# A drain behind the products of TensorE's walk: who raises the counts

## The reference, cut to what matters

```python
xn = layernorm(x)
# 1. graph part: mean over the neighbours, one product, norm
nsum = segment_sum(xn[src], dst, 6250);  deg = segment_sum(1, dst, 6250)
g = relu(concat([xn, nsum / max(deg, 1)]) @ W + b);  g = g / max(|g|, eps)
# 2. mixing: linear attention over all nodes, 4 heads of 32
q, k, v = split(rmsnorm(xn, g_pre) @ w_qkv)          # + 4 memory keys and values
q = softmax(q, over a head's 32) * scale;  k = softmax(k, over the nodes)
context = k^T v  (32 x 32 per head);  mix = rmsnorm((q context) @ w_out + b_out, g_out) + xn
x = x + g + mix
# 3. eight experts, the top two per node: gelu(ln(x) @ W1 + b1) @ W2 + b2, weighed and added
out = x + experts(layernorm(x))
```

## Time and profile before

| what | number |
|---|---|
| timed, median of 3 runs | 1981.92 us (1981.72 to 1984.41) |
| the profiled execution: its span | 2187.4 us |
| busy, share of that span: TensorE | 1583.7 us, 72% |
| VectorE | 1101.1 us, 50% |
| GpSimd | 1140.4 us, 52% |
| ScalarE | 900.9 us, 41% |

### The profile page before, as it was taken

How to read it: one execution, slowest core, us unless ns; L and a number is a source line. 1 busy time by engine, 2 the same in 40 slices (tenths; PEclk the granted TensorE clock), 3 DMA queues, 4 the chain that set the end, 5 groups by cost and what they waited for, 6 DMA issues and landing times.

```text
span 2187.4 us, 33907 instructions
## 1 busy us (share of the span) xinstructions
PE 1583.7 (72%) x9422; PEld 1361.2 (62%) x9423; DVE 1101.1 (50%) x3043; ACT 900.9 (41%) x1840; POOL 1140.4 (52%) x1141
## 2 busy tenths in 40 slices
PE   6735536546566667867767763548999999999998
PEld 5524435435454544545545543447999999999997
DVE  6512212212234536655555457765666666666664
ACT  6501101101112323323334336554666666666664
POOL 3267666666656666666666612555333333333333
PEclk9868868767878979988888785558999999999999
DMA  7334333333324655566656526537878777877775
GB/s 210 119 100 114 104 101 107 101 97 103 106 81 154 224 165 182 182 180 184 198 182 189 181 76 197 188 135 248 228 215 220 213 221 208 226 214 221 213 221 137
DMA packets 188123, 368.85 MB, mean 169 GB/s; under 512 B 33324, under 2 KB 134172, under 8 KB 173656
## 3 DMA queue, kind: packets, MB, share of 16 engines
q0 software_dynamic: 77296, 252.50, 41.3%
q1 hardware_dynamic: 102992, 113.64, 16.3%
q10 hardware_dynamic: 7736, 1.52, 0.4%
HBM read 287.94 MB, written 80.39 MB: 168 GB/s over the span
## 4 chain that ended last, share of the span: by engine, by line
PE 50%; another core or an unknown queue 17%; DVE 12%; issue 11%; DMA 5%; ACT 3%; SPq 2%; POOL 0%; DVEq 0%; ACTq 0%; POOLq 0%
PE bank L1813 11%; PE bank L2002 5%; PE bank L2003 5%; PE bank L2004 5%; PE bank L2025 5%; PE bank L2024 5%; PE bank L2026 5%; PE bank L1879 3%; DMA xTs<-xnT_d 3%; PE bank L1830 2%; PE bank L1973 1%; DVE acc_lent L1478 1%; DMA z_d<-w2s_lent 1%; DVE acc_lent L1307 1%
## 5 line engine op out<-in xcount | busy, mean ns | idle before, releaser
L695 POOL DMA_INDIRECT w2s_lent<-z_d,edge_tabs_lent x784 | 777.5, 992 | 438.7 <-issue 256.7
L1307 DVE TENSOR_TENSOR acc_lent<-acc_lent,bank 128x258 f32 x244 | 102.7, 421 | 600.6 <-remote 348.8
L1813 PE MATMUL bank<-w2s_lent,S_lent 128*128 x976 | 261.0, 416 | 19.0 <-issue 9.5
L1031 ACT ACTIVATE G<-bank,acc_lent 128x256 f32<-128x256 f32 x448 | 188.3, 472 | 205.9 <-DVE w2s L1670 124.5
L1813 PE MATMUL bank<-w2s_lent,G 128*128 x976 | 265.9, 422 | 3.4 <-issue 3.4
L2024 PE MATMUL bank<-w2s 128*128 128x256 f32 x896 | 264.4, 295 | 0.0
L2002 PE MATMUL bank<-w2s,acc 128*128 128x256 f32 x896 | 260.4, 291 | 2.8 <-issue 2.8
L739 POOL DMA_INDIRECT out_dram<-G,acc_lent x112 | 179.6, 1604 | 158.3 <-DVE G L1650 117.3
L1629 DVE TENSOR_TENSOR acc<-w1s,acc 128x512 fp32r<-128x512 f32 x224 | 155.1, 693 | 200.7 <-ACT acc L1000 174.1
L2004 PE MATMUL bank<-w2s,acc 128*128 128x256 f32 x896 | 254.0, 284 | 0.0
L2025 PE MATMUL bank<-w2s 128*128 128x256 f32 x896 | 253.7, 283 | 0.4 <-issue 0.4
(11 more groups left out here) (322 smaller groups left out, 2993.3 us busy)
## 6 DMA issues: line engine op xcount, KB each, us to landing
w2s<-w_d POOLq DMA_DIRECT2D x112, 1024.0 KB
w_d<-w2s_lent SPq DMA_DIRECT2D x64, 256.0 KB
acc_lent<-bucket_d SPq DMA_DIRECT2D x56, 266.0 KB
w2s_lent<-z_d,edge_tabs_lent POOLq DMA_INDIRECT x784
bu_d<-w2s_lent SPq DMA_DIRECT2D x98, 128.0 KB
w2s_lent<-bu_d SPq DMA_DIRECT2D x14, 768.0 KB
w1s<-in_L_ffn_W_dram SPq DMA_DIRECT2D x8, 1024.0 KB
w2s_lent<-in_L_ffn_W_dram SPq DMA_DIRECT2D x32, 256.0 KB
```

What stands on the lines that cost most here:

```text
L695: pool.indirect_dma_start(out=ring_rows[:, row % (RING * QUAD), 0:D], out_offset=None, in_=z_d[:, :], in_offset=bass.IndirectOffsetOnAxis( ...
L1031: g = act.activation(raw[q % 2][:, k * MT:(k + 1) * MT], bank[q][:, k * MT:(k + 1) * MT], ACT.Gelu, bias=b1c[1 - par][:, 2 * q + k:2 * q + ...
L1307: dve.tensor_tensor(to, to, bank[j % DEPTH][:, 0:ACCW], ALU.add).then_inc(s["acc_done"], 1)
L1813: m = pe.matmul(bank[j % DEPTH][:, 0:ACCW], S_of[j % DEPTH][:, k, :], rows[:, ds(bases[j], ACCW)], start=(k == 0), stop=(k == QUAD - 1))
```

## The change

A drain is an instruction in TensorE's stream that is done when all before it on that engine is done. At each of the places of the walk and the mixing where the last product of a group raised a semaphore, that product no longer does; a drain behind it does. All calls of `follow()` are left out (its function remains, without a caller). Nothing else changes: the same products in the same order, the same counts and waits. In the core of the diff (`turn_a`, `kv`, `ctx_mm`, `qu`, `bfold` and the turned biases are changed in the same way as `turn`; `kmaxrowT`, `ctxT` and `M2` as `kmaxT`):

```diff
@@ turn @@
                 for k in range(QUAD):
                     rows = ring[:, k * ACCW:(RING - 1) * QW_RING + (k + 1) * ACCW]
-                    m = pe.matmul(bank[j % DEPTH][:, 0:ACCW], S_of[j % DEPTH][:, k, :], rows[:, ds(bases[j], ACCW)],
+                    pe.matmul(bank[j % DEPTH][:, 0:ACCW], S_of[j % DEPTH][:, k, :], rows[:, ds(bases[j], ACCW)],
                                   start=(k == 0), stop=(k == QUAD - 1))
-                m.then_inc(s["p_ready"], 1)
-                if j < B_FIRST:
-                    follow()
+                pe.drain().then_inc(s["p_ready"], 1)
...
             def kv(t):
...
                 for c in range(DC):
-                    m = pe.matmul(bank[4][:, 0:2 * HID], xTs[:, c * P:(c + 1) * P], w_kv[:, c, :], start=(c == 0), stop=(c == DC - 1))
-                m.then_inc(s["kv_mm"], 1)
+                    pe.matmul(bank[4][:, 0:2 * HID], xTs[:, c * P:(c + 1) * P], w_kv[:, c, :], start=(c == 0), stop=(c == DC - 1))
+                pe.drain().then_inc(s["kv_mm"], 1)
...
-            pe.transpose(bank[6][:, 0:P], kmax, ident[:, :]).then_inc(s["kmaxT"], 1)
-            follow()
+            pe.transpose(bank[6][:, 0:P], kmax, ident[:, :])
+            pe.drain().then_inc(s["kmaxT"], 1)
...
             pe.matmul(bank[7][:, 0:D], ctxT, w_outs, start=True, stop=True)
-            follow(4)
+            pe.drain().then_inc(s["M2_mm"], 1)
...
             def turn_q(t):
                 pe.wait_ge(s["q_ready"], t + 1)
-                pe.transpose(bank[6][:, 0:P], q_s, ident[:, :]).then_inc(s["qT_mm"], 1)
+                pe.transpose(bank[6][:, 0:P], q_s, ident[:, :])
+                pe.drain().then_inc(s["qT_mm"], 1)
 
             def mix_out(t):
                 pe.wait_ge(s["qT_sb"], t + 1)
                 until(pe, s["o_evac"], t)
-                pe.matmul(bank[7][:, 0:D], qT_s, M2[:, :], start=True, stop=True).then_inc(s["o_mm"], 1)
+                pe.matmul(bank[7][:, 0:D], qT_s, M2[:, :], start=True, stop=True)
+                pe.drain().then_inc(s["o_mm"], 1)
```

More of the change, by code:

```diff
@@ L1822, in turn_a @@
                 for c in range(DC):
-                    m = pe.transpose(bank[5][:, c * P:(c + 1) * P], xr[:, c * P:(c + 1) * P], ident[:, :])
-                m.then_inc(s["xaT_mm"], 1)
+                    pe.transpose(bank[5][:, c * P:(c + 1) * P], xr[:, c * P:(c + 1) * P], ident[:, :])
+                pe.drain().then_inc(s["xaT_mm"], 1)
             def kv(t):
@@ L1843, in _ @@
             pe.wait_ge(s["kv_dve"], NT)
-            pe.transpose(bank[6][:, 0:P], kmax, ident[:, :]).then_inc(s["kmaxT"], 1)
-            follow()
+            pe.transpose(bank[6][:, 0:P], kmax, ident[:, :])
+            pe.drain().then_inc(s["kmaxT"], 1)
             pe.wait_ge(s["km_ready"], 1)
-            pe.transpose(bank[6][:, 0:P], kmaxb, ident[:, :]).then_inc(s["kmaxrowT"], 1)
-            follow()
+            pe.transpose(bank[6][:, 0:P], kmaxb, ident[:, :])
+            pe.drain().then_inc(s["kmaxrowT"], 1)
             pe.wait_ge(s["mk_exp"], 1)
@@ L1856, in ctx_mm @@
                 for j in range(nt):
-                    m = pe.matmul(bank[5][:, 0:HID + 2], ek[0:rows, j, :],
+                    pe.matmul(bank[5][:, 0:HID + 2], ek[0:rows, j, :],
                                   kv_all[0:rows, ds(8 * g + j, 1), HID:KVW].rearrange("p o w -> p (o w)"),
                                   start=False, stop=last, skip_group_check=True)
-                m.then_inc(s["ctx_mm"], 1)
+                pe.drain().then_inc(s["ctx_mm"], 1)
             for g in range(6):
@@ L1864, in _ @@
             ctx_mm(6, 1, TAIL, True)
-            follow()
             pe.wait_ge(s["ctx_ready"], 1)
-            pe.transpose(bank[6][:, 0:P], ctxs, ident[:, :]).then_inc(s["ctxT_mm"], 1)
-            follow()
+            pe.transpose(bank[6][:, 0:P], ctxs, ident[:, :])
+            pe.drain().then_inc(s["ctxT_mm"], 1)
             pe.wait_ge(s["ctxT_ready"], 1)
-            pe.matmul(bank[7][:, 0:D], ctxT, w_outs, start=True, stop=True).then_inc(s["M2_mm"], 1)
-            follow(4)
+            pe.matmul(bank[7][:, 0:D], ctxT, w_outs, start=True, stop=True)
+            pe.drain().then_inc(s["M2_mm"], 1)
             pe.wait_ge(s["M2_ready"], 1)
@@ L1878, in qu @@
                 for c in range(DC):
-                    m = pe.matmul(bank[4][:, 0:HID + D], xTs[:, c * P:(c + 1) * P], w_qu[:, c, :], start=(c == 0), stop=(c == DC - 1))
-                m.then_inc(s["qu_mm"], 1)
+                    pe.matmul(bank[4][:, 0:HID + D], xTs[:, c * P:(c + 1) * P], w_qu[:, c, :], start=(c == 0), stop=(c == DC - 1))
+                pe.drain().then_inc(s["qu_mm"], 1)
             def turn_q(t):
                 pe.wait_ge(s["q_ready"], t + 1)
-                pe.transpose(bank[6][:, 0:P], q_s, ident[:, :]).then_inc(s["qT_mm"], 1)
+                pe.transpose(bank[6][:, 0:P], q_s, ident[:, :])
+                pe.drain().then_inc(s["qT_mm"], 1)
             def mix_out(t):
@@ L1893, in bfold @@
                 for c in range(DC):
-                    m = pe.matmul(bank[5][0:EXPERTS, :], lnb[:, c, :], w1s[:, ds((e * DC + c) * HIDDEN + n * 512, 512)],
+                    pe.matmul(bank[5][0:EXPERTS, :], lnb[:, c, :], w1s[:, ds((e * DC + c) * HIDDEN + n * 512, 512)],
                                   start=(c == 0), stop=(c == DC - 1))
-                m.then_inc(s["bf_mm"], 1)
+                pe.drain().then_inc(s["bf_mm"], 1)
             for t in range(NT):
@@ L1913, in _ @@
                     for c in range(HC):
-                        m = pe.matmul(bank[5][:, c * EXPERTS:(c + 1) * EXPERTS], bacc[0:EXPERTS, c * P:(c + 1) * P], ident[0:EXPERTS, 0:EXPERTS],
+                        pe.matmul(bank[5][:, c * EXPERTS:(c + 1) * EXPERTS], bacc[0:EXPERTS, c * P:(c + 1) * P], ident[0:EXPERTS, 0:EXPERTS],
                                       start=True, stop=True)
-                    m.then_inc(s["b1_mm"], 1)
+                    pe.drain().then_inc(s["b1_mm"], 1)
             mix_out(NT - 1)
```

## The result

The changed kernel takes 2023.14 us (median of 4 runs, 2020.55 to 2029.48) against 1981.82 us before (4 runs, 1980.19 to 1984.41): 1.0216 times the time, 95% interval 1.0191 to 1.0240, or 41.3 us more. The forecast was 1992 us, 10 us more: the sign is right, and the loss is four times the forecast.

A forecast was written before the change was run, and what follows sets the result against it. The prediction took GpSimd's gathers to pace the walk; 4 us of lag left after mixing, 2 for the last chain and 4 of allowance made 10, on 1981.9: 1992 us. Its own range was 1986 to 2007, 8 in 10 1968 to 2035.

The forecast's parts named there:

- late counts: In the profiled walk before, TensorE's counts reached waiting engines late, once 39 us; the timed runs were taken to have few.
- The price of a drain: TensorE's cost per drain in walk and mixing: 0.44 us behind a turn, 0.36 behind another product.
- third cost: Sequencer work ahead of the next product now stands behind the drain: 0.13 us for a turn, 0.05 us elsewhere.
- fall by 23 x 0.9 to 4 at the end: Mixing's last 23 steps: TensorE's lag behind GpSimd falls 0.9 us a step, from 25 to 4 us.
- 16 x 1.3: Mixing's sixteen steps with a bfold: each takes TensorE 1.3 us more than the gathers, raising its lag from 4 to 25.
- C: Rival, chance 0.17: a drain is dearer, 0.6 us; mixing steps of 11.3 and 13.7 us add 63 us, 2045 us.
- A: Rival, chance 0.27: the gathers hide all of it at 0.31 us a drain; 1 to 2 us are left, 1983 us.
- B: Rival, chance 0.20: late counts cost something in the timed runs too, and drains' counts come in time: 1969 us.
- The tell-tale of C: Sign in the profile after that would show the dearer drain: GpSimd waits for L1813 through the mixing.
- where no gather runs: Stretch between the halves: counts come at once there, TensorE and the engines it waits for going round in 4.46 us.

The follow-up runs named there:

- e11: Kernel before with only two of a quad's four gathers from the ninth quad on: 1744.55 us, 0.8801 of the kernel before.
- e3: Kernel before without its 101 constant products and without any drain: 1979.92 us, 0.9991 of the kernel before.
- e1: Changed kernel with drains only up to the end of the stretch between the halves, no constant products: 1979.57 us, 0.9992 of the kernel before.
- e2: Kernel before, constant products kept, with drains raising the counts in the mixing only: 2022.64 us, 1.0223 of the kernel before.
- e7: Changed kernel with the register loads for the next eight turns issued ahead of the eighth turn's drain: 1992.55 us, 1.0072 of the kernel before.
- e9: Kernel before with drains only behind the mixing's products other than turns, register loads right behind every eighth turn's products: 1990.34 us, 1.0041 of the kernel before.
- e8: Changed kernel with two drains at each of the 517 places, the second raising the count: 2046.09 us, 1.0339 of the kernel before.
- e10: Kernel before without drains or constant products, register loads right behind the products of every eighth turn: 1981.48 us, 0.9989 of the kernel before.

## Why the prediction was wrong in size

**Right.** The walk before is paced by the gathers in the timed runs (e11), and the late counts of the profiled execution are not in them (e3 spans 1980.6 us). The first half hides its drains (e1). The removed products are worth nothing (e3). The loss is in the mixing (e2), and a drain takes 0.16 us of overlap from TensorE and adds 0.1 for a start on an idle engine. The drain itself is short: from the last product's end (1146.41) to the next sequencer instruction behind the drain (1146.53) it is 0.12 us in all.

**The step that failed** is "The price of a drain", in its third cost: "a register operation of 32 ns, a wait of 51 ns, another operation of 46 ns ... 0.13 us for a turn, 0.05 us elsewhere". I added the durations of the sequencer's instructions. Run one behind another on an empty TensorE they come 0.10 us apart, so that the gap is 0.42 us in front of a turn and 0.23 in front of qu and mix_out, against 0.18 and 0.10 in the sum. With the overlap and the start on an idle engine that makes 0.16 + 0.10 + 0.42 = 0.68 us for a drain between two turns, where 0.69 were measured and 0.44 forecast. And I let the register loads be half covered, 0.5 us per eight turns; they are wholly exposed, 1.72 - 0.42 = 1.30 us. A plain step came out at 10.35 + 3/8 x 1.30 = 10.84 us, not at 9.9.

**What hung on it.** The prediction let the lag "fall by 23 x 0.9 to 4 at the end": with 9.9 us a step TensorE was to win back its lag in the steps behind the last bfold. It doesn't. The qu products of the steps 0, 10, 26 and 48 cut the mixing as the sum did (after the steps 0, 10 and 26, the step 48 being the one at 1155.23 above; then 10, 26 and 48 of e3):

```profile
559.53 2.93 PE L1876 MATMUL bank<-w2s_lent,xTs 128*128 128x384 f32 x4 [0.54 <-DVE w2s_lent L1384]
...
677.76 1.53 PE L1876 MATMUL bank<-w2s_lent,xTs 128*128 128x384 f32 x4 [0.23 <-issue]
...
893.86 1.53 PE L1876 MATMUL bank<-w2s_lent,xTs 128*128 128x384 f32 x4 [0.23 <-issue]
```

```profile
677.13 2.26 PE L1872 MATMUL bank<-w2s_lent,xTs 128*128 128x384 f32 x3 [3.11 <-DMA w1s<-in_L_ffn_W_dram]
...
869.98 1.24 PE L1872 MATMUL bank<-w2s_lent,xTs 128*128 128x384 f32 x3
...
1114.62 1.56 PE L1872 MATMUL bank<-w2s_lent,xTs 128*128 128x384 f32 x4
```

The mixing starts 5.4 us later after (559.5 and 554.1), and behind the first ten steps the two are nearly level (677.8 and 677.1). The sixteen with a bfold take 216.1 us after and 192.9 in e3, 23 us more, against 21 in the forecast (16 x 1.3): that term was right by luck, as a dearer drain met a slower pace. The last 22 steps take 261.4 us (to 1155.23) against 244.6, 17 us more, where the forecast had 21 us less lag. A plain step of 10.84 us leaves only 0.3 us to the 11.1 us a step of e3, and in these steps TensorE still waits 11.7 us for tiles and 6.0 for gathers (e3: 30.2 and 19.8), so that nothing is won back.

So of the rivals C came nearest: it named 0.5 us a drain as the point from which plain steps no longer win time back, and six drains with the loads cost 10.84 - 7.29 = 3.55 us a step, 0.59 each. Its 63 us were too many: it put a plain step at 11.3 us, where 10.84 were measured, and took the pace of the mixing from the gathers alone, 10.8 us a step, where e3 takes (1114.62 - 554.1)/48 = 11.7. A was wrong, and B too (e1, 0.9992). The tell-tale of C, gathers that wait for the turns' drains, is in the profile after, but small (26.0 us; 7.3 for the same wait in e3):

```profile
POOL w2s_lent L695 <- PEq L1815: 26.0, 27, 7.8
```

**Open.** With the loads ahead, the drains still cost 13 to 14 us (e7), and those behind the other products 7 to 8 us (e9). They may be the rest of the sequencer's steps, or the longer chain through q; no run separates the two. Why counts came late in the profiled execution of before isn't known; it was not seen again. That they come at once "where no gather runs" is a misreading of the prediction's: in the 4.46 us that it names GpSimd runs two gathers, started at 633.39 and 635.04 us. No version with all its gathers is faster than before.

## What to carry to other kernels

A drain in TensorE's stream cost here, beside the lost overlap, what the sequencer then had to do in the open: count the instructions behind it (waits, register operations, loads of registers) and price each by the distance from one to the next (0.10 us here), not by its duration. Put register loads ahead of the drain (e7: 27 to 28 of 41 us back). A stage paced by another engine forgave such a price up to its slack (e1), and where the slack was gone it charged nearly all of a further one (e8: some 24 of 25 us).

## What was not expected of the hardware

TensorE's sequencer passes one small instruction in about 0.10 us when nothing covers it, though they last 0.03 to 0.05 us (a second drain: 13 ns long, 0.08 us of gap). Two register loads of 0.59 us are free behind queued products (in e3 15 of the 19 turns of the mixing that load registers start without a gap, the other four wait for a gather, and e10 gains nothing) and cost 1.30 us behind a drain.
